# In-projection of a Mamba-attention-MoE kernel that reads its input joint by joint, and one activation table for exp and ln

## What is computed

```python
xr = jnp.transpose(x, (0, 2, 1, 3)).reshape(N * J, T, C)   # joint by joint
xz = jnp.einsum('btc,ec->bte', xr, W_in)                   # in-projection, 128 -> 512
xc, z = jnp.split(xz, 2, axis=-1)
xp = jnp.pad(xc, ((0, 0), (D_CONV - 1, 0), (0, 0)))
xw = jnp.stack([xp[:, k:k + T, :] for k in range(D_CONV)], axis=-1)
xc = jnp.einsum('btdk,dk->btd', xw, conv_w) + conv_b       # 4 taps along time
xc = jax.nn.silu(xc)
x_dbl = jnp.einsum('btd,ed->bte', xc, W_xproj)             # dt_in, B, C
dt = jax.nn.softplus(jnp.einsum('btr,dr->btd', dt_in, W_dt) + b_dt)
dA = jnp.exp(jnp.einsum('btd,ds->btds', dt, A))
dBu = jnp.einsum('btd,bts->btds', dt * xc, Bm)
# scan over t: h = dA_t * h + dBu_t ; y_t = sum_s h * C_t
y = (y + xc * D_skip) * jax.nn.silu(z)
out = jnp.einsum('btd,cd->btc', y, W_out)                  # then an RMS norm, + residual
```

## Time and profile before

| what | us |
|---|---|
| median of 3 runs | 1722.59 (1722.4 to 1724.98) |
| profiled execution, first to last instruction | 1723.2 |
| DVE busy | 1338.4 (78%) |
| PE busy | 1238.6 (72%) |
| ACT busy | 1110.6 (64%) |
| POOL busy | 701.9 (41%) |

### The profile page before, as it was taken

The page is one execution under the profiler, slowest core; times in us unless marked ns, Lnnn a source line. Parts: engine busy times, 40 slices in busy tenths (PEclk is TensorE's granted clock), DMA queues, the critical chain, the costliest instruction groups (busy, mean ns, idle before and its releaser), DMA issues. The chain is left out here.

```text
span 1723.2 us, 22121 instructions
## 1 busy us (share of the span) xinstructions
PE 1238.6 (72%) x7264; PEld 550.1 (32%) x7264; DVE 1338.4 (78%) x2280; ACT 1110.6 (64%) x2041; POOL 701.9 (41%) x399
## 2 busy tenths in 40 slices
PE   5124588868887688777886888588848873884994
PEld 3001432243224322432243224332323232322683
DVE  4898789888988889788979997899778972602465
ACT  4332767777776778677967686769676863682430
POOL 3464245524562356235623562346333641000265
PEclk9556788977898889878996899689968996896997
DMA  2540534145414641372228131824063404001562
GB/s 65 174 138 29 190 70 155 38 154 135 154 33 151 144 144 39 128 171 99 85 67 228 61 127 42 209 88 144 18 183 79 164 20 84 32 1 38 163 182 70
DMA packets 94023, 185.11 MB, mean 107 GB/s; under 512 B 15512, under 2 KB 48564, under 8 KB 93908
## 3 DMA queue, kind: packets, MB, share of 16 engines
q1 hardware_dynamic: 92500, 180.41, 35.2%
q0 software_dynamic: 1408, 3.29, 0.6%
HBM read 146.47 MB, written 36.86 MB: 106 GB/s over the span
## 5 line engine op out<-in xcount | busy, mean ns | idle before, releaser
L1274 DVE TENSOR_TENSOR_SCAN hst<-dA,PS 128x800 f32<-128x800 f32 x256 | 466.2, 1821 | 38.5 <-ACT dA L939 5.6
L1001 ACT ACTIVATE probs<-PS 128x400 f32<-128x400 f32 x800 | 343.0, 533 | 61.7 <-PE PS L1573 61.6
L939 ACT ACTIVATE dA<-dt_rep,a_sb 128x775 f32<-128x775 f32 x256 | 244.7, 959 | 78.6 <-DVE hst L1274 53.4
L1573 PE MATMUL PS<-q_stack,k_stack 99*128 99x400 bf16 (+1 forms) x896 | 238.5, 356 | 76.8 <-ACT probs L1001 51.0
L1269 DVE TENSOR_TENSOR PS<-u_rep,b_rep 128x800 f32<-128x800 f32 x256 | 267.6, 1045 | 14.1 <-DMA u_rep<-u_dram 2.3
L991 ACT ACTIVATE probs<-PS 128x400 f32<-128x400 f32 x400 | 200.4, 503 | 107.6 <-PE PS L1540 90.3
L1294 DVE CUSTOM_DVE_ANT_0 probs<-PS,probs 128x400 f32<-128x400 f32 x400 | 220.4, 574 | 41.6 <-issue 29.0
L796 POOL TENSOR_TENSOR sp_l<-hst,c_rep 128x800 f32<-128x800 f32 x72 | 135.6, 1883 | 196.2 <-DVE PS L1269 196.1
L1558 PE MATMUL PS<-probs,v_ext 128*32 128x400 f32 (+1 forms) x1792 | 206.9, 540 | 5.6 <-ACT probs L1001 5.6
L796 POOL TENSOR_TENSOR dt_sb<-hst,c_rep 128x800 f32<-128x800 f32 x72 | 135.7, 1884 | 110.8 <-DVE PS L1269 78.5
L1539 PE MATMUL PS<-k_stack,q_stack 96*128 96x400 bf16 (+1 forms) x448 | 152.0, 375 | 39.9 <-DVE k_neg L1253 37.5
(11 more groups left out here) (225 smaller groups left out, 2110.0 us busy)
## 6 DMA issues: line engine op xcount, KB each, us to landing
b_rep<-b_dram SPq DMA_DIRECT2D x64, 400.0 KB, 4.4
c_rep<-c_dram SPq DMA_DIRECT2D x64, 400.0 KB, 4.0
dt_rep<-dt_dram SPq DMA_DIRECT2D x64, 400.0 KB, 6.4
u_rep<-u_dram SPq DMA_DIRECT2D x64, 400.0 KB, 6.5
q_stack<-parts_dram SPq DMA_DIRECT2D x96, 100.0 KB, 4.3
k_stack<-parts_dram SPq DMA_DIRECT2D x96, 100.0 KB, 5.3
dt_dram<-dt_sb SPq DMA_DIRECT2D x16, 400.0 KB, 3.4
u_dram<-sp_l SPq DMA_DIRECT2D x16, 400.0 KB, 3.8
```

The lines of the kernel that those rows point to most:

```text
L939: nc.scalar.activation(dA[:, i % NDA, :].rearrange("p (j t) -> p j t", t=T)[:, :, 1:T], dt_rep[:, gi, :].rearrange("p (j t) -> p j t", t=T ...
L1001: nc.scalar.activation(probs[:, j % NPROB, :], bank(4 + j % 3, HALF), ACT.Exp, scale=ATT_SCALE).then_inc(probs_ready.sem, 1)
L1274: nc.vector.tensor_tensor_scan(hst[:, i % 2, :], dA[:, i % NDA, :], dbu, 0.0, ALU.mult, ALU.add).then_inc(scan_done.sem, 1)
L1573: last = nc.tensor.matmul(bank(4 + j % 3, HALF)[strip], k_stack[:, h, kt * P:kt * P + strip.stop - strip.start], q_stack[:, h, q0:q0 + HAL ...
```

## The change

`project_in` reads `xnT` joint by joint: the moving operand of its two matmuls is a view (j t) of the tile, 16 joints by 32 times and 9 joints by 32 times, in which neighbours lie 25 elements of 4 bytes apart. So PSUM holds x and z in the order (j t). The convolution's three shifted taps become views of 25 runs, since a step back in time is now one element within a joint: 31, 30 and 29 elements a run. The silus lose their transposing views and read and write 800 elements in one run. Behind the last silu of z an explicit table load is put in for the set `natural_log_exp_and_others`, which has Exp and Ln; the build then finds both functions in the loaded set.

```diff
--- before.py
+++ after.py
@@ -832,13 +832,6 @@
             def norm(f):
                 pass
 
-            def in_jt(ap):
-
-                return ap.rearrange("p (j t) -> p t j", j=J)
-
-            def by_tj(ap):
-                return ap.rearrange("p (t j) -> p t j", j=J)
-
             def norm_apply(tiles, src, dst):
                 for k in range(NT):
                     last = nc.scalar.activation(dst[:, k, :], src[:, k, :], ACT.Identity, scale=tiles["r"][:, 1, k:k + 1],
@@ -854,13 +847,13 @@
                         else:
                             act.wait_ge(y_summed.sem, y_summed.at(m, NC_))
                     act.wait_ge(conv_done.sem, conv_done.at(f, ck + 1))
-                    nc.scalar.activation(in_jt(xc[:, ck, :]), by_tj(sp_e[:, ck, :]), ACT.Silu).then_inc(silu_done.sem, 1)
+                    nc.scalar.activation(xc[:, ck, :], sp_e[:, ck, :], ACT.Silu).then_inc(silu_done.sem, 1)
 
                 def silu_z(ck):
                     if m is not None:
                         act.wait_ge(y_ready[ck].sem, y_ready[ck].at(m, 1))
                     act.wait_ge(xz_up.sem, xz_up.at(f, NC_ + ck + 1))
-                    nc.scalar.activation(in_jt(z_act[:, ck, :]), by_tj(wide(0)), ACT.Silu).then_inc(silu_done.sem, 1)
+                    nc.scalar.activation(z_act[:, ck, :], wide(0), ACT.Silu).then_inc(silu_done.sem, 1)
 
                 def absolute(ck):
                     act.wait_ge(dt_up.sem, dt_up.at(f, ck + 1))
@@ -880,6 +873,7 @@
                     act.wait_ge(xd_up.sem, xd_up.at(f, 1))
                     nc.scalar.copy(xd[:, :], wide(2)).then_inc(xd_ready.sem, 1)
                     silu_z(1)
+                    nc.scalar.preload_act_table_set("natural_log_exp_and_others")
                     absolute(0)
                     exp_of(f, 0)
                     ln_of(f, 0)
@@ -1132,9 +1126,10 @@
                     fthen(nc.vector.tensor_scalar(sp_e[:, ck, :], src, conv_w_sb[:, ck, TAPS - 1:TAPS],
                                                   conv_b_sb[:, ck:ck + 1], ALU.mult, ALU.add))
                     for back in range(1, TAPS):
+                        later = by_jt(sp_e[:, ck, :])[:, :, back:T]
                         ins = nc.vector.scalar_tensor_tensor(
-                            sp_e[:, ck, back * J:], src[:, 0:TOK - back * J],
-                            conv_w_sb[:, ck, TAPS - 1 - back:TAPS - back], sp_e[:, ck, back * J:], ALU.mult, ALU.add)
+                            later, by_jt(src)[:, :, 0:T - back],
+                            conv_w_sb[:, ck, TAPS - 1 - back:TAPS - back], later, ALU.mult, ALU.add)
                         if back < TAPS - 1:
                             fthen(ins)
                     ins.then_inc(conv_done.sem, 1)
@@ -1437,7 +1432,10 @@
                 pe.wait_ge(weights_in, NW[0])
 
             def project_in(b, e):
-                return over_spans(b, w_in_sb[:, e * P:(e + 1) * P], xnT)
+                for at, width in SPANS:
+                    last = nc.tensor.matmul(PS[:, b * BANK + at:b * BANK + at + width], w_in_sb[:, e * P:(e + 1) * P],
+                                            in_tj(xnT[:, :])[:, at // T:(at + width) // T, :], start=True, stop=True)
+                return last
 
             def front(n, m, f):
                 def out_project(tiles):
```

## The result

The changed kernel takes **1746.49 us** (median of four runs, 1738.16 to 1750.83) against 1722.49 of the kernel before beside it (1721.00 to 1724.98): a ratio of 1.0141, interval [1.0118, 1.0165]. It is slower by 24 us. The forecast was 1712; the rival of the slow reads had said 1742. The profiled execution of the changed kernel took 1738.16, its fastest, so the trace shows the lower end of the loss: a span of 1736.4 against 1723.2, 13 us.

A forecast was written before the change was run, and what follows sets the result against it. No engine was full; the front's chain through PE, ACT and DVE to L1148 was taken as the bound. The first front's 2.1 us plus seven others at 1.15 gave 10.2 us off 1722.6: 1712.4, range 1705 to 1725.

The forecast's parts named there:

- the rival of the slow reads: In-projection: PE reads strided float32 at half rate, 1.4 us more a projection, 2.8 us a front, 1742 us; chance 0.15.
- in-projection's strided moving operand: Four projections a front read xnT with a 100-byte step; the forecast took no added time.
- upper end of 1.4: In-projection: a strided access doubles the time, as with silu and product, so 1.4 us more a projection.
- The lower end: In-projection: nothing added, since strided weight loads took 0.89 ns a column and a projection streams at 0.90.
- the same engine and a read: Reason for trusting PE's weight-load row for the in-projection over silu and product, which are writes; nothing added.
- or on PE's queue, which is 0.7 us earlier: Rest of the front's path, including the wait for the squares, was taken to hang on L1148 or PE's earlier queue.
- silus 0.87: All four silus of a front, written contiguously, take 0.87 us, 0.7 less each; only two lie on the chain.
- L1143 behind L1190: DVE step after the Abs (L1148 behind L1195 before the change): bound by L1195, it starts 1.15 us earlier a front.
- the first front: Front with no scan ahead, both chunks on ACT: 2.1 us gained, with 1.15 and 3.3 as ends.
- The taps in 25 runs: Convolution's three tap instructions on DVE: taken as costing nothing, with 1.6 us over eight fronts as the end.
- The table load by itself: Load ahead of Exp only moves past the Abs; kernel before with it alone stays within 0.2%, 1720 to 1725.
- That a stretch of scans gives gains back: Rival: all six full scan stretches last 140.46 us, giving 9.5 us back, 1721.9 us; chance 0.10.

The follow-up runs named there:

- the other kernel: A separate kernel that copies x to the output and times strided and contiguous TensorE reads and weight loads alone; float32 read 0.43 us contiguous, 0.92 with step 25.
- GpSimd copy: Changed kernel plus a second tile that GpSimd fills joint by joint from xnT once a turn, read contiguously by the in-projection: 1715.11 us, ratio 0.9945 to the kernel before.
- contiguous reads: Changed kernel with the in-projection reading xnT in one run of 800 columns, the reorder left out: 1711.47 us against 1723.03 of the kernel before, ratio 0.9938.

## Why the prediction was wrong

**The step that failed** is the in-projection's strided moving operand: "strided reads would just keep up ... I take nothing". It costs 1.58 us a projection, over the upper end of 1.4 that I had set beside it. The upper end rested on the right row: the silu and the product of the earlier trace rows pay for SBUF, not for writing, and the silus that read with a stride show it. The lower end rested on the earlier trace rows: I took the surplus of the strided load over a contiguous one, 35 ns, and added it to the contiguous rate, 0.89 ns a column. That surplus is no price of a read: where reads were all that ran, a strided load cost 1.0 ns a column more, and the matmul's own read went from 0.84 to 1.8 ns an element. Nor did the loads of the earlier trace rows show such a rate. Here are the matmuls that use them, in the front of the earlier trace rows, at a clock of 1.00:

```profile
335.40 1.99 PE L1625 MATMUL PS<-ident,o_raw 128*100 128x128 f32 x16
...
348.73 1.08 PE L1483 MATMUL PS<-ident,part_rest 128*100 128x128 f32 x8
```

The 16 with strided weights take 1.99 us, the 8 with contiguous ones 1.08: 0.12 and 0.13 us each. These loads overlap other work, so a longer duration says nothing of what it costs, and here the step cost nothing; why these loads keep up and those of the other kernel don't stays open. The argument that set the row above the others ("the same engine and a read") was the wrong way to choose: all three rows touch SBUF with a step, and two of them showed the doubling.

**The rival's walk held, with a price somewhat low.** It put the second x-projection 2.6 us behind the forecast's place, which was 0.74 ahead of the old one, so 1.9 us later than before. Measured are 2.5; with 1.58 instead of 1.4 its sum gives 2.4 (3 x 1.58 - 1.6 - 0.74). For a front it said 2.8, and with 1.58 it gives 3.6. L1143 came 3.4 later, and the six fronts grew by 3.7 to 4.1, like with like. Of the difference 0.35 are the squares at L1196, which I had let hang on L1148 "or on PE's queue, which is 0.7 us earlier": PE's queue was later. Its 1742 stands against 1746.5, with a chance of 0.15, and the range had left it out.

**The rest held in the world without the strided read.** Forecast 10.2 us, measured 11.6 by medians (the interval of 0.9938 is 6.5 to 14.8). Point by point, in that kernel's trace: silus 0.87, as forecast; L1143 behind L1190, as forecast, and 1.39 us earlier instead of 1.15, since the Abs comes 0.18 earlier than before (I had it where it was) and L1143 starts 0.97 behind L1190, not 1.06 (the Abs I put at 355.03 adds up to 355.01, which changes nothing); the first front 1.63 us shorter instead of 2.1. The taps in 25 runs cost nothing (998 ns median). The table load by itself costs 0.03% [-0.18, 0.24]: nothing, as forecast. Behind shorter silus it may be worth more than I knew: with the GpSimd copy the eight fronts take 310.6 us with the load and 318.4 without. Of these 7.9 us, like with like, 1.6 lie in the first, 0.5 in each of fronts 1 to 6 and 0.3 in the last; 2.8 lie in two stars more.

**What stays open:** the front behind the first turn shrank by 3.0 us (38.81 to 35.84) with contiguous reads and the last, starred in both, by 1.10; I followed the like ones only. Before, the first of these holds the stretch at 0.50 from 14.9 us on, and with contiguous reads it does not. The GpSimd copy, traced twice, had such a stretch in one trace only, with 37.54 us there against 35.84; by this estimate 1.7 of the 3.0 belong to the clock, and 1.3 are left, near the 1.39 of the like ones. The 1.10 of the last is not explained. That a stretch of scans gives gains back was not seen with contiguous reads (1077.1 against 1077.7). The GpSimd copy's stretches are longer, but so are some without a copy, which I haven't resolved.

## What to carry to other kernels

Where a reorder must happen, try it where VectorE or ScalarE reads PSUM: with a step of 25 float32 that cost nothing here, while the same step in SBUF made an operation 1.9 to 2.5 times as long, whether read or written, and TensorE's moving operand 2.1 times. The duration of an instruction that overlaps others is no rate; the way from start to start is, and only where nothing else limits it. Of rows that disagree on an access that no row shows, the pessimistic one belongs in the range. A change of several parts is worth splitting: here three parts gained 12 us and one lost 33.

## What the runs showed of the hardware

- TensorE reads a moving operand of 512 float32 columns in 0.43 us in a run, 0.45 with a step of 2, 0.68 with 3, 0.90 with 4, 0.92 with 25. The strided price is one of elements: bf16, 0.23 us with step 2, costs 0.88 with a step of 25.
- The strided read doesn't follow TensorE's clock (float32 0.92 us at 1.00, bf16 0.88 at 0.50), the contiguous one does (float32, 0.43 at 1.00, 0.85 at 0.50).
- On 800 float32 a step of 25 in SBUF takes VectorE from 0.70 to 1.76 us, ScalarE from 0.87 to 1.69, GpSimd from 0.85 to 1.67 or 1.69, read or written; in PSUM VectorE stays at 1.11 and ScalarE at 0.84.
- A front that begins at a granted clock of 0.50, for less than 1.1 us, ends up to 1.6 us later.
